# New order inside the step, and on POOL the solve of two chunks ahead of both chunks' scatters

## What is computed

```python
q = (x @ Wq); k = (x @ Wk); v = (x @ Wv); beta = sigmoid(x @ Wb)      # 4 heads, 128 keys, 32 values
k = k * rsqrt(sum(k*k) + 1e-12); q = q * 128 ** -0.5
for t in range(n):                                                    # delta rule
    delta = (v_t - k_t^T S) * beta_t
    S = S + k_t delta^T ; o_t = q_t^T S
o = o * rsqrt(mean(o*o) + 1e-5) * norm_w * silu(x @ Wg)
x = layernorm(x + o @ Wo)
w = softmax(x @ gate_w.T); top 2 of 8 experts, each takes at most 640 slots of a row of 2048 tokens
x = layernorm(x + sum over the two experts of w_e * (silu(x w1_e) * (x w3_e)) w2_e)
```

## Time and profile before

| what | us |
|---|---|
| median of 3 runs (lowest, highest) | 529.44 (528.06, 533.39) |
| the profiled execution's own time | 533.86 |
| its span, first to last instruction | 532.1 |
| PE busy (matmuls) | 474.0 (89%) |
| ACT, POOL, DVE busy | 327.8, 325.0, 318.2 |
| granted TensorE clock, mean | 0.96 |

### The profile page before, as it was taken

One profiled execution on the slowest core, in us unless ns is written; L12 is line 12 of the kernel. 1 busy time (PEld: TensorE's weight loads), 2 busy tenths in 40 slices (PEclk: granted clock), 3 DMA queues, 4 the chain that ended last, 5 costly groups with the idle time before them and its releaser, 6 DMA issues.

```text
span 532.1 us, 19041 instructions
## 1 busy us (share of the span) xinstructions
PE 474.0 (89%) x7181; PEld 390.5 (73%) x7181; DVE 318.2 (60%) x1209; ACT 327.8 (62%) x905; POOL 325.0 (61%) x445
## 2 busy tenths in 40 slices
PE   6979988999999999999979877999999999999910
PEld 4656765777667776676656567999999999999910
DVE  4435457767777677767855682654455654555445
ACT  2545767877878778787744643555555555555464
POOL 3052717857688676886865543476676766767752
PEclk9998999999999999999985999999999999999965
DMA  3368754673554835548183224254536545453376
GB/s 94 28 112 201 224 142 51 72 121 40 75 49 60 106 28 74 50 58 107 14 171 41 29 32 111 42 109 56 121 46 129 110 55 109 79 107 35 31 148 198
DMA packets 154804, 46.10 MB, mean 87 GB/s; under 512 B 107168, under 2 KB 149280, under 8 KB 154720
## 3 DMA queue, kind: packets, MB, share of 16 engines
q1 hardware_dynamic: 132848, 29.86, 28.7%
q0 software_dynamic: 20288, 9.51, 19.6%
q10 hardware_dynamic: 1584, 5.59, 2.7%
HBM read 21.39 MB, written 23.55 MB: 84 GB/s over the span
## 4 chain that ended last, share of the span: by engine, by line
PE 44%; POOL 24%; issue 14%; DMA 9%; SPq 4%; DVE 3%; ACT 1%; DVEq 0%; ACTq 0%; POOLq 0%
PE ps L1004 18%; POOL slots_in L1744 11%; PE ps L1015 11%; POOL xs L1727 5%; POOL prod L1726 5%; PE ps L1030 2%; PE ps L681 2%; DMA a_diag<-hb 2%; PE ps L962 2%; POOL silu L1752 1%; SPq L541 1%; DMA inv<-xs 1%; DMA xi<-inv 1%; DMA ssd<-a_diag 1%; DMA xTs<-xT 1%
## 5 line engine op out<-in xcount | busy, mean ns | idle before, releaser
L1785 POOL DMA_INDIRECT x_store<-xk,row x80 | 124.7, 1559 | 66.3 <-ACT xk L1275 46.8
L1744 POOL DMA_INDIRECT slots_in<-x,slot x64 | 99.2, 1550 | 23.7 <-issue 17.1
L1603 DVE TENSOR_TENSOR hb<-ps,hs 128x320 f32<-128x320 f32 (+1 forms) x128 | 62.5, 491 | 47.7 <-ACT hs L1267 43.2
L1267 ACT ACTIVATE hs<-ps 128x320 f32<-128x320 f32 (+1 forms) x128 | 55.3, 435 | 32.1 <-PE ps L1004 27.3
L1004 PE MATMUL ps<-xeTh,w13h 128*128 128x320 f32 x224 | 70.5, 315 | 1.0 <-DVE xeTl L1627 1.0
L1004 PE MATMUL ps<-xeTh,w13l 128*128 128x320 f32 x224 | 69.1, 309 | 0.0
L1004 PE MATMUL ps<-xeTl,w13h 128*128 128x320 f32 x224 | 69.1, 309 | 0.0
L1015 PE MATMUL ps<-w2s,hb 128*128 128x128 f32 x512 | 64.5, 279 | 0.7 <-DVE hb L1603 0.7
L1015 PEld LDWEIGHTS ps<-w2s,hb 128*128 128x128 f32 x512 | 59.8, 192 | 3.1 <-DVE hb L1603 1.1
L1275 ACT ACTIVATE xk<-ps,gs 128x128 f32<-128x128 f32 x80 | 24.2, 364 | 45.0 <-PE ps L1030 35.3
L1726 POOL TENSOR_TENSOR prod<-a,xs 128x28 f32<-128x28 f32 (+11 forms) x120 | 33.3, 278 | 23.8 <-DVE xs L1437 14.9
(11 more groups left out here) (218 smaller groups left out, 1149.4 us busy)
## 6 DMA issues: line engine op xcount, KB each, us to landing
slots_in<-zeros ACTq DMA_DIRECT2D x10, 520.0 KB, 4.0
xe<-slots_in SPq DMA_DIRECT2D x15, 325.0 KB
w<-w_in SPq DMA_DIRECT2D x8, 448.0 KB
xTs<-xT SPq DMA_DIRECT2D x4, 512.0 KB, 5.5
a_diag<-hb SPq DMA_DIRECT2D x64, 32.0 KB
inv<-xs SPq DMA_DIRECT2D x16, 128.0 KB
xi<-inv SPq DMA_DIRECT2D x16, 128.0 KB
xk<-x SPq DMA_DIRECT2D x8, 256.0 KB, 4.3
```

The lines of the kernel that those rows point to most:

```text
L1267: af(hs[to, s % 4, :], ps[src, HB[fill_of(s) % 5], 0:HALF], ACT.Silu).then_inc(hs_ready, 1)
L1603: v.tensor_tensor(hb[to, par, c, HALF * g:HALF * g + HALF], ps[rows_, at, 0:HALF], hs[rows_, s % 4, :], ALU.mult).then_inc(h_ready, 1)
L1744: g.indirect_dma_start(out=xs_d[:, :], out_offset=bass.IndirectOffsetOnAxis(ap=to, axis=0), in_=x1[:, p % 2, j, k, :], in_offset=None, com ...
L1785: g.indirect_dma_start(out=x1_d[:, :], in_=ye[:, par, i, :], in_offset=None, out_offset=bass.IndirectOffsetOnAxis(ap=row[:, par, i:i + 1], ...
```

## The change

It writes the calls of a step in another order on PE, ACT and DVE, and on POOL it does a chunk's scatter only in odd steps, for two chunks together and behind the solve.

```diff
             for p in range(NP + LAST):
                 at(turn_keys, p - 5)
                 at(project, p - 6)
-                at(z_128, p - 5)
                 if p == NP + 5:
                     keep_on(9)
                 key_pair(p - 1, p - 5, 0)
+                at(z_128, p - 5)
+                at(queries, p - 4, 0)
                 at(w_128, p - 5)
-                at(queries, p - 4, 0)
                 at(gate_in, p - 4)
+                key_pair(p - 1, p - 5, 1)
                 at(deltas, p - 5)
-                key_pair(p - 1, p - 5, 1)
                 at(state_queries, p - 5)
+                at(queries, p - 4, 1)
                 at(turn_deltas, p - 5)
-                at(queries, p - 4, 1)
...
+                at(key_key_out, p - 3, 0)
                 at(z128_copy, p - 7)
-                at(key_key_out, p - 3, 0)
+                at(queries_out, p - 6, 0)
                 at(t128_copy, p - 7)
-                at(queries_out, p - 6, 0)
-                at(deltas_out, p - 7)
                 at(gate_out, p - 6)
                 at(x1_rstd, p - 8)
                 at(key_key_out, p - 3, 1)
-                at(deltas_turned, p - 7)
+                at(deltas_out, p - 7)
...
                 at(queries_out, p - 6, 1)
+                at(deltas_turned, p - 7)
                 at(softmax, p - 8)
...
                 at(state_copy, p - 6)
+                at(gated_values, p - 6)
                 at(z64_copy, p - 5)
-                at(keys_read, p - 5)
-                at(gated_values, p - 6)
                 if p - 6 == NP - 1:
                     w_low(0, 0, 0)
+                at(keys_read, p - 5)
                 at(gated_out, p - 6)
                 if p - 6 == NP - 1:
                     w_low(0, 0, 1)
+                at_group(scale_blocks, p - 2)
+                if p == 2:
+                    solve_first()
                 at(t64_copy, p - 5)
                 at(x64_turned, p - 5)
+                at(masked, p - 5, 0)
                 at(residues, p - 5)
...
-                at_group(scale_blocks, p - 2)
-                if p == 2:
-                    solve_first()
-                at(masked, p - 5, 0)
                 at(normalise, p - 6)
...
                 at(silu_of, p - 2)
-                at(scatter, p - 4)
+                if p % 2:
+                    at(scatter, p - 5)
+                    at(scatter, p - 4)
```

## The result

The changed kernel takes 535.06 us (median of 20 runs, 530.69 to 539.04). The kernel before, measured beside it, takes 528.81 us (median of 20, 525.78 to 533.39). The ratio is 1.0101, 95% interval 1.0077 to 1.0126: slower by 5 to 6 us. The ratios here leave out executions more than 1.5% above the fastest of their kernel, so they differ a little from the quotient of the medians. I had forecast 527.1 us, with 533.5 as the upper end.

What follows compares the result with a forecast made beforehand. It took the steady part as bound by PE's own stream, with only small waits to win. Order -3.6, hand-over +0.3 and last scatters +1.0 sum to -2.3, set on the median 529.44: 527.1 us, range 518.5 to 533.5.

Steps and rivals of the forecast that it cites:

- I take 0.3 a step: Steady steps, new order: waits before project and z_128 go, 0.20 a step comes at outputs; -3.6 us over twelve steps.
- The wait at outputs: Steady steps: with queries(1) ahead of turn_deltas, PE waits for ACT before outputs (L881), 0.20 us a step.
- a like wait may come at w_128: Steady steps: ACT copies a key block ahead of z128_copy, so PE may wait 0 to 0.15 us at w_128.
- The solve ahead of both scatters: POOL's last solve begins 4.3 us earlier, at 251.0; inverse_in at 268.8; the 2.26 us wait at z_32 goes.
- what is late next: Hand-over: chunk 10's scatter lands at 275.7 beside the expert weights, x1_out(12) waits, project_x starts at 276.9; +0.3 us.
- The last scatters: End of stage: chunks 12, 13 and 14 scatter in a row from 298.57, until 321.0; +1.0 us, ends 0 and +2.0.
- Setting the sum on the median: The profiled execution was 4.4 us above the median, so -2.3 was applied to the median 529.44, giving 527.1.
- the steady steps slow down: Rival, steady steps: late-landing scatters hold x1_out on DVE, up to 1.5 us a pair; +6.7, 536.1 us; chance 0.12.
- The order gives nothing: Rival, steady steps: removed waits return at w_128 and outputs, 0 instead of -3.6; +1.3 in all, 530.7 us; chance 0.18.
- The tail opens: Rival, hand-over: chunk 10 lands early, PE stands under 2 us and keeps 2.4 GHz; -11.1, 518.3 us; chance 0.15.

Runs made afterwards that it cites:

- e4: The changed kernel with 54 instead of 36 products of keep_on at the end of the stage: 534.77 us, ratio 1.0122.
- e1: The kernel before with only POOL's change, both chunks' scatters behind the solve, step order as before: 546.9 us, ratio 1.0336.
- e12: The kernel before with POOL's pairs of scatters and, of the new order, only scale_blocks ahead of t64_copy on DVE: 543.59 us, ratio 1.0274.
- e2: The changed kernel with a scatter in every step of POOL, so the new order alone: 531.64 us, ratio 1.0047.
- e5: The changed kernel with pairs until POOL's step 13, then single scatters from step 14: 529.36 us, ratio 1.0019.
- e6: The changed kernel with single scatters from POOL's step 16; chunk 10 stays behind the last solve, chunk 12 goes in idle time: 531.87 us, ratio 1.0045.
- e7: The changed kernel with chunks 10 and 11 scattered alone in steps 14 and 15, chunks 12 to 15 back to back: 534.75 us, ratio 1.0110.
- e13: The changed kernel with SP's two loads of expert weights one step later: 532.27 us, ratio 1.0069.
- e8: e5 with the order of before in the second half of the step on PE and ACT: 533.04 us, ratio 1.0077.
- e9: e5 with z128_copy ahead of key_key_out(0) on ACT: 526.68 us, ratio 0.9943.
- e10: e9 with the two keys_out ahead of t_diag on ACT: 528.69 us, ratio 1.0027.
- e11: e10 with a scatter in every step of POOL, as in the kernel before: 530.95 us, ratio 1.0032.
- e17: e9 with the expert weights loaded one step later: 525.55 us, ratio 0.9959.
- e15: The changed kernel with single scatters from POOL's step 16, expert weights one step later, z128_copy first on ACT: 526.95 us, ratio 0.9939.
- e16: The kernel before with the expert weights loaded one step later, nothing else: 530.61 us, ratio 0.9998.
- e18: The kernel before, unchanged, run for a third profile: 528.41 us, where its median on that chip was 527.86.

## Why the prediction was wrong

| run | edit, in a word | ratio to before |
|---|---|---|
| the change | order and pairs | 1.0101 |
| e4 | change, more keep_on | 1.0122 |
| e1 | pairs alone | 1.0336 |
| e12 | pairs, scale_blocks early | 1.0274 |
| e2 | order alone | 1.0047 |
| e5 | order, singles from step 14 | 1.0019 |
| e6 | change, chunk 12 in the idle time | 1.0045 |
| e7 | change, chunk 10 ahead of the last solve | 1.0110 |
| e13 | change, weights later | 1.0069 |
| e8 | e5 with the late swap undone | 1.0077 |
| e9 | e5 with z128_copy first | 0.9943 |
| e10 | e9 with keys_out ahead of t_diag | 1.0027 |
| e11 | e10 with single scatters | 1.0032 |
| e17 | e9 with weights later | 0.9959 |
| e15 | e6 with weights later and z128_copy first | 0.9939 |
| e16 | kernel before, weights later | 0.9998 |

By the ratios, and taking 529 us for the kernel before, the loss adds up: order of the step +2.5 (1.0047), pairs in the steady part -1.5 (1.0019 - 1.0047, not sure), hand-over and end of the stage +4.3 (1.0101 - 1.0019). Together +5.3. I had -3.6, 0, and +0.3 + 1.0.

The profiles cut at the starts of z_32 (L751) in chunks 3, 12, 14 and 15 and at the load (L608) show the same parts, in us:

| profile | 3 to 12 | 12 to 14 | 14 to 15 | 15 to load |
|---|---|---|---|---|
| before, first | 150.30 | 30.47 | 20.97 | 28.94 |
| before, usual (e18) | 149.62 | 30.42 | 16.52 | 27.53 |
| the change | 152.01 | 28.26 | 20.57 | 30.30 |
| chunk 10 late alone (e6) | 150.61 | 27.99 | 21.06 | 26.72 |
| four in a row alone (e7) | 150.68 | 31.15 | 16.05 | 30.32 |
| neither (e5) | 151.22 | 31.39 | 15.81 | 26.72 |

The late chunk 10 saves about 3 us ahead of z_32 of chunk 14 and loses 5 behind it; the four in a row cost 3.6 in the last column. The third column holds the stretch at 0.50 too: from the top 17.07, 6.83, 10.24, 10.24, 6.83 and 6.83 us.

- *"I take 0.3 a step. Twelve steps run in full: -3.6 us"* is the first failed step. The removed waits did go. The wait at outputs was about as priced: 1.9 us in nine steps, 0.21 a step for 0.20. But I wrote "a like wait may come at w_128 ... 0 to 0.15" and did not put it in the sum; it came with 0.21 or more in eight of the nine steps, 2.1 us. And I did not ask what z_128 had covered for the key pair: 0.38 a step at L730. Waits of 1.01 in a pair became 7.4 / 4.5 = 1.64. My price list began from the waits that the change removes; it should have begun from the operations that it brings forward, and asked for each what its inputs wait for.
- I held the order as one part that helps or does not. The runs show parts with opposite signs: ACT's z128_copy behind key_key_out costs 4 us (2.7 by the medians), the late swap earns 3, and the early scale_blocks without the key pair ahead of z_128 makes 8.6 us of stands there (e12).
- *The solve ahead of both scatters, and what is late next*: right in mechanism, and the size is in part luck. The solve began at 250.21 (forecast 251.0), inverse_in at 267.94 (268.8), the landing came at 275.3 (275.7), project_x at 276.45 (276.9), and the cause of the late landing, the weights beside it, is shown. But 1.3 us of this execution were won ahead of the last steps; counted from z_32 of chunk 12 the term is +1.2 and not +0.3, and as a cost to the whole it was +1.4 where it stood alone.
- *"The last scatters ... +1.0 us"* is the second failed step. The queue itself was right: 22.35 forecast from chunk 12 to chunk 15, 22.60 measured. What it was compared with was wrong. I took 298.57 and 320.01 from the first profile of before. In a usual execution these are 293.45 and 313.49, and the same sum from there gives 293.45 + 22.6 - 313.49 = +2.6; two runs side by side show +3.6 to the start of chunk 15 and +4.8 in the time. In the first profile 17 us at 1.2 GHz had made PE late, and POOL with it. The end that I gave as 0 to +2.0 did not hold it either.
- *Setting the sum on the median*, 529.44 - 2.3, did this without saying so: the sum held for an execution with the long slow stretch. The 15.8 us at 0.50 in the earlier trace rows were the place of the 4.4 us by which that execution lay above the median, and I kept them for both kernels.
- Of the rivals, "the steady steps slow down" (536.1) was nearest in number, which is luck: x1_out waited once for a scatter in the steady part, 1.21 us at 174.62. It is what the pairs do without the new order (e1). "The order gives nothing" (530.7) was nearest in mechanism and still 4 us short. "The tail opens" needs the weights later, and even then it came in one of two executions (e13, and not e15).

Left open: why the run with 54 of keep_on shows a shorter expert stage in its profile and no gain in time, why the stretch at 0.50 differs so in length between executions, and whether the pairs in the steady part are worth anything.

## What to carry to other kernels

When a step is reordered, make the list from the operations brought forward: for each, which engine writes its input and when, by the timeline. A group that waits is often the cover of the next one's wait.

Before you price the end of a stage, find where the profiled execution lost what it has over the median. A stretch at the lower clock there makes another engine the late one and hides what the usual run will pay; a second and third profile of the unchanged kernel would have shown it.

A group that is moved into a queue costs its length less the gaps that the queue had there; so ask which gaps are there in the usual execution.

## What was not expected of the hardware

- After nearly the same stand of PE (2.26, 2.56 and 2.53 us) at the same place, the same kernel stayed at the 1.2 GHz level for 17.07, 17.07 and 6.83 us. With 2.49 us in a kernel that differs in one load it was 13.65. From z_32 of chunk 14 to that of chunk 15 these three executions took 20.97, 20.07 and 16.52 us, so this place alone moves an execution by about 4 us, just under 1% of the time.
- The scatters of the last chunk, which write and do not add, take 0.95 to 1.01 us each on POOL, those that add 1.54 to 1.92. In the code the two differ by the DMA's compute_op.
- A transfer that adds into DRAM and shares the DMA engines with the expert weights lands 2.7 us later than without them (4.7 against 2.0 after the end of its issue; in three further profiles 5.2 and 5.3 with them, 2.4 without).
